# Nine one-hot tables in place of ten, a third raw tile and spaced loads of the weights in a recommendation tower

## The reference

```python
e = jnp.stack([tbl_0[ids[:, 0]], ..., tbl_25[ids[:, 25]]], axis=1)   # 2048 x 26 x 128
combined = jnp.concatenate([e, r_dense_x[:, None, :]], axis=1)
interact = jnp.einsum('bfd,bgd->bfg', combined, combined)
z = interact[:, _TRIU_I, _TRIU_J]                                    # 351 pairs
h = jnp.concatenate([z, r_dense_x], axis=1)
h = jnp.maximum(h @ W_top1 + b_top1, 0.0)                            # 479 x 512
h = jnp.maximum(h @ W_top2 + b_top2, 0.0)                            # 512 x 256
y = h @ W_top3                                                       # 256 x 1
```

## Time and profile before

| | |
|---|---|
| median of 3 runs | 479.07 us |
| the runs | 476.82 to 482.74 us |
| profiled execution, time | 478.38 us |
| profiled execution, span | 476.6 us |
| TensorE busy, mean granted clock | 433.7 us (91%), 0.989 |
| VectorE, ScalarE, GpSimd busy | 306.9, 234.6, 247.8 us |
| moved by DMA | 30.97 MB, mean 65 GB/s |

### The profile page before, as it was taken

One profiled execution on the slowest core, in us unless ns is written; L12 is line 12 of the kernel. 1 busy time (PEld: TensorE's weight loads), 2 busy tenths in 40 slices (PEclk: granted clock), 3 DMA queues, 4 the chain that ended last, 5 costly groups with the idle time before them and its releaser, 6 DMA issues.

```text
span 476.6 us, 9175 instructions
## 1 busy us (share of the span) xinstructions
PE 433.7 (91%) x3464; PEld 409.3 (86%) x3464; DVE 306.9 (64%) x495; ACT 234.6 (49%) x796; POOL 247.8 (52%) x264
## 2 busy tenths in 40 slices
PE   0768989799999999899799999999999999979978
PEld 0767979689999989889799999899999999969866
DVE  4999384754787557874489657783599556922251
ACT  2553645945445444545346354455446354543543
POOL 6555346655655666566554566566556565630000
PEclk9999999999999999999999999999999999987999
DMA  5773621212122122221122122221222222110000
GB/s 175 230 206 87 173 60 54 56 45 63 51 60 57 48 64 62 53 62 55 52 61 58 51 60 57 56 63 47 57 59 59 59 57 61 40 33 2 0 3 0
DMA packets 25452, 30.97 MB, mean 65 GB/s; under 512 B 6361, under 2 KB 18273, under 8 KB 25408
## 3 DMA queue, kind: packets, MB, share of 16 engines
q0 software_dynamic: 8192, 16.79, 12.8%
q1 hardware_dynamic: 16336, 12.79, 9.7%
q10 hardware_dynamic: 880, 0.80, 0.6%
HBM read 30.35 MB, written 0.01 MB: 64 GB/s over the span
## 4 chain that ended last, share of the span: by engine, by line
PE 80%; DVE 9%; ACT 5%; issue 4%; another core or an unknown queue 0%; ACTq 0%; DVEq 0%
PE x_ps L512 30%; PE gram_ps L526 23%; PE tail_ps L580 15%; DVE onehot L682 5%; PE x_ps L499 5%; PE tail_ps L559 3%; DVE hot_lo L669 3%; PE tail_ps L550 2%; PE tail_ps L586 2%; ACT gram L333 1%; ACT xt L315 1%; DVE gram L333 1%; ACT z L347 1%; ACT xt L648 1%; ACT weights_hi L658 1%
## 5 line engine op out<-in xcount | busy, mean ns | idle before, releaser
L482 POOL DMA_INDIRECT raw<-in_tbl,ids_sb x256 | 246.9, 965 | 175.9 <-issue 92.5
L682 DVE TENSOR_TENSOR onehot<-ids_wide,row_ps 128x1024 fp32r<-128x1024 int16 (+1 forms) x184 | 205.5, 1149 | 44.5 <-PE x_ps L512 34.2
L512 PE MATMUL x_ps<-onehot,hot_hi 128*128 128x256 f32 x688 | 184.5, 302 | 28.3 <-DVE onehot L682 20.3
L512 PE MATMUL x_ps<-onehot,hot_lo 128*128 128x256 f32 x688 | 172.0, 282 | 0.0
L512 PEld LDWEIGHTS x_ps<-onehot,hot_hi 128*128 128x128 f32 x688 | 130.8, 190 | 37.5 <-issue 26.4
L526 PE MATMUL gram_ps<-xt 128*128 128x108 f32 x1024 | 136.4, 280 | 5.3 <-ACT xt L648 3.6
L526 PEld LDWEIGHTS gram_ps<-xt 128*128 128x128 f32 x1024 | 126.6, 195 | 8.2 <-ACT xt L648 4.0
L512 PEld LDWEIGHTS x_ps<-onehot,hot_lo 128*128 128x128 f32 x688 | 131.0, 190 | 0.0
L333 ACT COPY gram<-gram_ps 32x104 f32<-32x104 f32 x288 | 68.3, 237 | 91.5 <-PE gram_ps L526 78.7
L333 DVE COPY gram<-gram_ps 32x104 f32<-32x104 f32 x224 | 59.9, 268 | 56.6 <-PE gram_ps L526 47.5
L315 ACT COPY xt<-x_ps 128x128 f32<-128x128 f32 (+1 forms) x110 | 49.4, 506 | 54.4 <-PE x_ps L512 42.5
(11 more groups left out here) (36 smaller groups left out, 278.8 us busy)
## 6 DMA issues: line engine op xcount, KB each, us to landing
ids_wide<-in_hot_ids SPq DMA_DIRECT2D x80, 64.0 KB
raw<-in_tbl,ids_sb POOLq DMA_INDIRECT x256
hot_in<-in_tbl SPq DMA_DIRECT2D x14, 256.0 KB, 3.1
hot_in<-in_tbl SPq DMA_DIRECT2D x6, 320.0 KB, 3.8
weights_in_place<-in_w SPq DMA_DIRECT2D x3, 256.0 KB
dense_sb<-in_dense_t ACTq DMA_DIRECT2D x6, 128.0 KB
dense_sb<-in_dense_t SPq DMA_DIRECT2D x2, 128.0 KB
w1d_sb<-in_w SPq DMA_DIRECT2D x1, 256.0 KB
```

The costliest lines, as they stand in the source:

```text
L482: nc.gpsimd.indirect_dma_start(out=raw[k][:, f, :], out_offset=None, in_=sources[f], in_offset=bass.IndirectOffsetOnAxis(ap=ids_sb[:, t, f ...
L512: last = nc.tensor.matmul(ps, table[:, chunk_at[j] + c, :], columns(p)[:, c - a, :], start=(c == 0 and table is hot_hi), stop=(c == chunks ...
L682: nc.vector.tensor_tensor(columns(p), ids_wide[:, it % IDS, 0:width].unsqueeze(1).to_broadcast([P, n, width]), row_no[chunks[j]][:, a:b].u ...
```

## The change

HOT goes from 10 to 9: one table of 1250 rows is no longer a one-hot table but is gathered. That makes 17 gathers a tile in 5 turn groups (3, 3, 4, 3 and 4 tables), 272 in all in place of 256, and a block of 9 items in 20 pieces, 76 chunks, 152 matmuls at line 512. RAW goes from 2 to 3. The knob LEAVE, which would gather further tables in the last block only, is added and stays 0, as LATE does; with both at 0 the lines that speak of `BOTH` and `used` change nothing.

The order changes in three places. Beside the odd tile's products stand 6 pieces in place of 8 (`beside`), and ahead of them, after the first block, the list runs to the end of an item (`lead`). The turns of the next even tile stand at the ends of the remaining items. In the last block that has one-hot work (block 7's pieces) these turns stand one item earlier each, so that two are done behind the products of tile 13 and three behind the 8-chunk table's, and the three pieces of the last table come between them and the products of tile 14. Before, the last two turns stood directly ahead of those products.

The weights' loads begin one row of ids later and go out one behind each row in place of two; their casts stand beside the `gram` steps 12 to 16. ScalarE's copy of the dense vectors to `xt` is placed by the middle of the block's items. The host code sorts the tables accordingly.

```diff
--- before.py
+++ after.py
@@ -15,9 +15,11 @@
 SLOTS = 32
 QUAD = 4
 BANK = 512
-HOT = 10
+HOT = 9
 LATE = 0
-RAW = 2
+LEAVE = 0
+BOTH = max(LATE, LEAVE)
+RAW = 3
 DENSE = 2
 RING = 3
 PIECE = 4
@@ -53,8 +55,9 @@
     row_kinds = sorted(set(chunks))
 
 
-    sources = tables + hot_tables[:LATE]
-    gathered = [nf + LATE if t < tiles_block else nf for t in range(tiles)]
+
+    sources = tables + hot_tables[:BOTH]
+    gathered = [nf + (LATE if t < tiles_block else LEAVE if t >= tiles - tiles_block else 0) for t in range(tiles)]
     turn_groups = []
     for n in gathered:
         count = -(-n // 4)
@@ -99,7 +102,7 @@
     def is_last(t, f):
         return gather_no[t, f] % BURST == BURST - 1
 
-    def landed(t, g, last, upto=nf + LATE):
+    def landed(t, g, last, upto=nf + BOTH):
 
         return 16 * sum(is_last(u, f) == last for u in range(t % RAW, t + 1, RAW) if g < len(turn_groups[u])
                         for f in turn_groups[u][g] if u < t or f <= upto)
@@ -109,9 +112,9 @@
         return sum(len(turn_groups[u]) for u in range(t % RAW, t, RAW)) + g + 1
 
 
-    used_from = {j: 1 if j < LATE else 0 for j in range(nh)}
-    hot_order = list(range(LATE, nh)) + list(range(LATE))
-    items = [(j, h * tiles_block, tiles_block) for h in range(blocks) for j in hot_order if used_from[j] <= h]
+    used = {j: range(1 if j < LATE else 0, blocks - 1 if j < LEAVE else blocks) for j in range(nh)}
+    hot_order = list(range(BOTH, nh)) + list(range(LATE, BOTH)) + list(range(LATE))
+    items = [(j, h * tiles_block, tiles_block) for h in range(blocks) for j in hot_order if h in used[j]]
     split_no = {j: n for n, j in enumerate(hot_order)}
     first_item = {j: min(it for it, item in enumerate(items) if item[0] == j) for j in range(nh)}
     pieces, item_end = [], []
@@ -121,6 +124,7 @@
         pieces += [(it, cut[i], cut[i + 1]) for i in range(count)]
         item_end.append(len(pieces))
     item_start = [0] + item_end[:-1]
+    j_th = [n for h in range(blocks) for n in range(len([j for j in range(nh) if h in used[j]]))]
     last_item = [max(it for it, (_, first, n) in enumerate(items) if first <= t < first + n) for t in range(tiles)]
 
     def hot_pieces(t):
@@ -156,22 +160,30 @@
             held = item_end[pieces[hot[0][0][1]][0]] - hot[0][0][1]
             slots += hot[:held] + gram_slots(t)
             slots[-1].append(("held", pieces[hot[0][0][1]][0]))
-            lead = n_gram if h > 0 else len(hot) - n_gram
+            rest_pieces = len(hot) - held
+            beside = rest_pieces * 8 // 21
+            lead = held + rest_pieces * 6 // 21 if h > 0 else len(hot) - beside
+            while h > 0 and hot[lead - 1][0][1] + 1 not in item_end:
+                lead += 1
             ends = [end + 1 for end in item_ends(hot[held:lead])[:-1]]
             slots += with_turn(slots[-1:] + hot[held:lead], t + 1, [0] + ends if h > 0 else ends[-2:])[1:]
         else:
             slots += gram_slots(t) + with_turn([[] for _ in turn_groups[t + 1]], t + 1, list(range(len(turn_groups[t + 1]))))
-            lead = 0
+            lead, beside = 0, 0
         if h > 0:
             tail_to.append(len(slots))
-        slots += gram_slots(t + 1, hot[lead:lead + n_gram])
+        slots += gram_slots(t + 1, hot[lead:lead + beside])
         tail_from.append(len(slots))
         if h == 0:
             n = len(turn_groups[t + 2])
             slots += with_turn([[] for _ in range(n_gram + n)], t + 2, [n_gram + g for g in range(n)])
         elif hot:
-            rest_slots = hot[lead + n_gram:]
-            slots += with_turn(rest_slots, t + tiles_block, item_ends(rest_slots))
+            rest_slots = hot[lead + beside:]
+            ends = item_ends(rest_slots)
+            if h < blocks - 2:
+                slots += with_turn(rest_slots, t + tiles_block, ends)
+            else:
+                slots += with_turn(slots[-1:] + rest_slots, t + tiles_block, [0] + [end + 1 for end in ends[:-1]])[1:]
     held_items = [step[1] for slot in slots for step in slot if step[0] == "held"]
     for h in range(blocks - 1):
         at = COVER_START
@@ -219,8 +231,8 @@
             return ctx.enter_context(nc.semaphore(name))
 
         ident = sb("ident", [P, P])
-        ids_sb = sb("ids_sb", [P, tiles, nf + LATE], I32)
-        raw = [sb(f"raw{k}", [P, nf + LATE, P]) for k in range(RAW)]
+        ids_sb = sb("ids_sb", [P, tiles, nf + BOTH], I32)
+        raw = [sb(f"raw{k}", [P, nf + BOTH, P]) for k in range(RAW)]
         xt = sb("xt", [P, XT * P, SLOTS])
         dense_sb = [sb(f"dense_sb{k}", [P, BLOCK]) for k in range(DENSE)]
         y_sb = sb("y_sb", [1, BLOCK])
@@ -256,7 +268,7 @@
         weight_parts = [[t[0:n, k, :] for t in (w1z_hi, w1z_lo, w1z_at)] for k, n in enumerate(kz)]
         weight_parts += [[t[:, k:k + 2, :] for t in (w2_hi, w2_lo, w2_at)] for k in range(0, m1, 2)]
         n_weights = n_kz + 6
-        weights_at_gram = range(gram_block - len(weight_parts), gram_block)
+        weights_at_gram = range(gram_block + 1 - len(weight_parts), gram_block + 1)
 
         x_ps = [psum(f"x_ps{b}", [P, BANK]) for b in range(3)]
         row_ps = psum("row_ps", [P, BANK])
@@ -452,12 +464,11 @@
                 ids_load(it)
                 if it == early + 2:
                     dense_load(1)
-                at = 2 * (it - early - IDS + 1)
-                for n in range(max(at, 0), max(at + 2, 0)):
-                    if n < 2 * LATE:
-                        half_load(2 * early + n)
-                    elif n < 2 * LATE + n_kz + 3:
-                        weights_load(n - 2 * LATE)
+                n = it - early - IDS
+                if 0 <= n < 2 * LATE:
+                    half_load(2 * early + n)
+                elif 0 <= n < 2 * LATE + n_kz + 3:
+                    weights_load(n - 2 * LATE)
             sp.wait_ge(y_stored, 16 * blocks)
 
         @block.gpsimd
@@ -621,7 +632,7 @@
                     act.wait_ge(xt_cleared, 1)
 
                 to_xt(copy, first, n, nf + j, x_ps[fill_no["hot", it] % len(x_ps)]).then_inc(x_copied, 1)
-                if it == last_item[first] - nh // 2:
+                if it == (it - j_th[it] + last_item[first] + 1) // 2:
                     h = first // tiles_block
                     act.wait_ge(dense_in[h % DENSE], (h // DENSE + 1) * 16)
                     to_xt(copy, first, tiles_block, nf + nh, dense_sb[h % DENSE]).then_inc(dense_copied, 1)
@@ -718,7 +729,7 @@
     batch, n_tables = inputs["ids"].shape
     rows = [inputs[f"tbl_{f}"].shape[0] for f in range(n_tables)]
     hot = sorted(range(n_tables), key=lambda f: rows[f])[:HOT]
-    hot = hot[HOT - LATE:] + hot[:HOT - LATE]
+    hot = hot[HOT - BOTH:] + hot[:HOT - BOTH]
     cold = [f for f in range(n_tables) if f not in hot]
 
     order = cold + hot + [n_tables]
@@ -731,7 +742,7 @@
     ids = np.asarray(inputs["ids"])
     arrays = {
         "dense_t": inputs["r_dense_x"].T,
-        "ids": ids[:, cold + hot[:LATE]].reshape(batch // P, P, len(cold) + LATE).transpose(1, 0, 2),
+        "ids": ids[:, cold + hot[:BOTH]].reshape(batch // P, P, len(cold) + BOTH).transpose(1, 0, 2),
 
         "hot_ids": np.ascontiguousarray(ids[:, hot].T).view(np.int16)[:, ::2],
         "w1": np.concatenate([w1[pair_rows], w1[len(pair_rows):]]),
```

## The result

The changed kernel takes 484.42 us (median of 4 runs, 483.3 to 485.15) beside 477.94 us for the kernel before (4 runs, 475.15 to 482.74): 1.015 times, interval 1.009 to 1.021. The forecast was 476.5 us. The profiled execution takes 485.15 us for a span of 483.2.

A forecast was written before the change was run, and what follows sets the result against it. The gather chain was taken to become the bound from tile 1: last gather landed 444.4, plus 1.6 lateness and 28.0 end, span 474.0; with 1.8 and 0.7 added, 476.5 us. Range 468 to 485, 8 in 10.

The forecast's parts named there:

- The direct price: Gather chain: sixteen more gathers, 25.4 us, against 22.5 us by which the last gather lands before its turn on TensorE.
- the three terms that shorten the chain: Gather chain: 2.2, 3.5 and 1.5 us off, putting the last gather's issue at 441.8.
- (a): Start: the tenth table's two loads, 640 KB, leave, so a burst waits less; 2.2 us saved, bounds 1 and 3.
- (b): Start: weights' loads spaced one behind each row of ids delay gather bursts less; 3.5 us saved, between nothing and 7.
- (c): Whole gather chain: nine rows of ids per block in place of ten; 1.5 us saved, bounds 0 and 2.4.
- A fall after tile 14's last turn: TensorE waits 4.6 us before that turn, then runs at the low clock, costing 5.1 us.
- the 1.6 us of lateness: End: TensorE reaches tile 15's last turn 1.6 us after its data, because of the low clock.
- The first: Rival: gathers land quicker and aren't the bound, TensorE alone decides; 459 us, or 451 without gap and low clock; chance 0.1.
- The second: Rival: spaced weights' loads hold up more bursts in the start, a saving of 3.5 becomes +5; 484.3 us; chance 0.2.
- The third: Rival: no fall before tile 15's last turn, then one in the closing products, 5.1 us longer; 479 to 481; chance 0.2.
- TensorE alone: TensorE's own end if gathers never held it: 457.5 us, or 449.6 with block 7's turns moved.
- The table's leaving: One-hot work gone: 2.1 us less on TensorE for each of 7 blocks, 14.7, plus 4.35 on VectorE in the first.

The follow-up runs named there:

- idle gather: Kernel before plus a seventeenth gather per tile that repeats the first table's and is never read: 492.14 us, 1.053 of the kernel before.
- group waits: GpSimd waits only for the turn group two back, descriptor ring enlarged: changed kernel 447.29 us (0.959 of the kernel before), kernel before 456.78 us (0.978).
- weights in pairs: Changed kernel with the weights' loads two by two behind rows of ids, casts one product earlier: 492.31 us, 1.054 of the kernel before.
- wide loads: Changed kernel with the first layer's three weight blocks each loaded as 128 rows: 485.12 us, 1.044 of the kernel before.
- old order: Changed kernel with the order list built as before, all three places undone: 488.7 us, 1.047 of the kernel before.

## Why the prediction was wrong

**Right: the mechanism.** The gathers are a chain of their own, paced by landings and not by buffers; the cover is used up and the chain becomes the bound from tile 1 on. The idle gather and the group waits show it from both sides. RAW = 3 is worth nothing while the burst waits stand. Tile 15's last turn comes 2.56 us after its gather, and from there to the end of the span it is 27.9 us (28.0 forecast). The direct price, sixteen gathers less the cover, 25.4 - 22.5 = 2.9 us, stood too: at 1.609 a gather it is 3.2.

**Wrong: the three terms that shorten the chain**, -7.2 us in the sum, which turned a loss into a gain; they came to +3.9. The time lies inside the stated 468 to 485, but at its upper end, and the last gather (452.79, said 438 to 447) and tile 2's first (71.50, said 60 to 67) lie outside theirs. (a) and (b) together were put at -5.7 and measured at -1.4. Ahead of the first load of weights, where (b) can't act yet, the twenty-second gather goes out at 45.80 before and 45.00 after, and on the second chip at 46.11 and 43.01: (a) is -0.8 and -3.1. That leaves about -0.6 for (b) on both chips, where -3.5 was put down; with the weights in pairs tile 2 begins at the same time. The rule of the Trainium skill on the number of engines was weighed and set aside for a middle value; the wide loads bear it out. (c), fewer rows of ids, was put at -1.5, and the change of the step that should have shown it is on the first chip +5.3 (237 steps of 0.022 more). Put together these give 423.55 + 25.4 - 1.4 + 5.3 = 452.9 for the last gather, which was at 452.79; that is bookkeeping, since both terms are read from that chain. On the second chip the start gained 3.8, the step changed by nothing (1.610 and 1.608), and the change lost more all the same, since the cover was small.

The error of (c) is one of kind. Rows of ids do cost about what the term took for all of them, 14 us (1.5 for a tenth). But a tenth fewer of them was not a tenth less waiting. The bursts of the first chip, counted as above, point elsewhere: in the kernel before 32 of 74 meet a row of ids alone and wait 1.37 us, 12 meet an instruction fetch and wait 1.69, 26 meet neither and wait 1.05. Over the bare wait the rows cost some 10 us in both kernels; the bursts with fetches cost 8 us before and 12 after, and on the second chip 11 and 9. What the fetches are worth was not tried in any run. My reading, argued and not shown, is that a burst is late by where in it the broadcast falls (single bursts that met one waited between 1.0 and 2.6 us), and that this shifts with everything else. Between the six traced kernels with burst waits and seventeen whole gathers a tile (without the old order) the step runs from 1.608 to 1.638 and between the three with sixteen from 1.587 to 1.610, in executions whose traffic is nearly the same. What moves it inside these ranges was not found. A margin of some 0.03 us a gather, 7 us on this chain, belonged to the range; with it the forecast's sign was open, and why the step rose by 0.022 on the first chip stays open.

**The clock.** A fall after tile 14's last turn came as forecast, but shorter: 3.4 us at the low level, not 10.2, so it cost 1.7 us of work and TensorE was at tile 15's last turn when its data was; the 1.6 us of lateness did not occur. That the low clock is paid out of later waits and not at the end held on the first chip: seven stretches, 30.7 us at half speed, are 15 us of TensorE's work, and the end is where the gathers put it, 2.56 + 27.9 us after the last issue. On the second chip it was 3.37 + 31.0, with a stretch at 0.50 in the end; the kernel before has its 31.0 there too, so this is no part of what the change costs. By the Trainium skill (TensorE: Matmul & The Clock Gate, "HAM oscillation") matmuls that wait for DMA again and again start at the low clock every time. On the first chip the falls behind the waits of 1.87 to 5.84 us agree with it; on the second the clock stayed at 1.00 behind waits of 2.97 and 3.14 us, so "every time" is not borne out. This is the changed kernel's window there behind the second of them:

```profile
318.00:324.00 6.00, 5.94 (x51) 5.23 (x50) 4.22 (x8) 2.67 (x10) 2.83 (x3) 1.00 0.25 59
```

**The rivals.** The first (landing gets quicker) is out. The second, weights spaced out that hold up more bursts, had the right sign and gave 484 us, which the time hit (484.42), but by luck and not by its mechanism: its (b) of +5 was -1.4 with (a), and the loss came in the later steps. Its sentence on one narrow load was right. The third is out on the first chip: tile 14's wait was followed by a fall, and none came in the closing products.

**TensorE alone** was put at 449.6 with block 7's turns moved. With the gathers out of the way the span is 444.8, on another chip; 2.9 us more than on the first go into its end (30.9 us, with 6.8 of it at the low clock). The table's leaving saved about 10 us of span (455.2 to 444.8) where 19 were put down. In the start 4.35 us were counted and 1.8 came by tile 3's last turn (116.79 and 114.95). My reading, not shown, is that with and without the table tile 1's turns come first. From there to tile 15's last turn it is 308.9 and 298.9 us, 10.0 for six blocks, 1.7 a block where 2.1 were put down. The end takes 1.4 us of it back (29.6 and 30.9).

## What to carry to other kernels

An engine that is half idle can be a chain with its own clock: divide the distance of its first and last instruction by their count, and compare the time it would need for the new count with the cover it has at the end, before counting what the bound engine saves. The cover differed between the traced executions on two chips (22.5 and 3.6 us here), so a trade that uses it up costs more where the other engine runs well. If a chain waits for landings, widen what may be in flight before changing how much work goes over it: here that edit is worth 8 to 9% in the changed kernel (447.29 and 488.9 us) and made the traded table worth 2%. With more in flight, look again at the buffers, which were free before.

## What the runs showed of the hardware that was not expected

The wait for a gather's landing grows by 0.4 us when a broadcast of 64 KB runs between, at a mean DMA share of 0.2, and by 0.7 when an instruction fetch does; cutting these broadcasts to an eighth brought 14 to 21 us to a chain of 237 gathers. Behind a load of 118 rows of 2 KB a burst of gathers waited 5.99 us, behind one of 128 rows 2.70. Gathers that wait only for the turn group two back go out every 1.27 us in the mean, with up to some eight in flight, where with burst waits it is 1.61.
